# Loading every second chunk of a statistics pass from GpSimd's DMA queue

## What is computed

```python
def reference(x, w):
    v = group_norm(x)                       # 32 groups: 2 channels x 256 x 256 pixels share mean and variance
    vc = clip(v, -8, 8)
    s = max(abs(vc)).max() / 127            # ONE scale for the whole tensor
    vq = clip(round(vc / s), -127, 127) * s
    ws = mean(abs(w), per output channel)
    wq = clip(round(w / ws), -1, 1) * ws    # ternary weights
    return x + conv1x1(vq, wq)
```

## Time and profile before

| what | value |
|---|---|
| median of 3 runs | 1880.15 us (1879.89 to 1880.23) |
| the profiled execution, its own time | 1879.99 us |
| span of the profile, first to last instruction | 1878.2 us |
| busy: DVE, ACT, PE, POOL | 88%, 58%, 55%, 22% of the span |
| DMA | 797.09 MB, mean 424 GB/s over the span |
| mean granted clock of TensorE | 0.672 of full speed |

### The profile page before, as it was taken

How to read it: one execution, slowest core, us unless ns; L and a number is a source line. 1 busy time by engine, 2 the same in 40 slices (tenths; PEclk the granted TensorE clock), 3 DMA queues, 4 the chain that set the end, 5 groups by cost and what they waited for, 6 DMA issues and landing times.

```text
span 1878.2 us, 9814 instructions
## 1 busy us (share of the span) xinstructions
PE 1036.2 (55%) x2237; PEld 332.6 (18%) x2237; DVE 1646.0 (88%) x956; ACT 1085.4 (58%) x796; POOL 417.1 (22%) x139
## 2 busy tenths in 40 slices
PE   0999999999999644444434334333343333433342
PEld 0333333333333211111100000000000000000000
DVE  4999999999999999999988888888888888888885
ACT  0999899899899755455444443444434444344432
POOL 0676776767767300000000000000000000000000
PEclk9999999999999855555555555555555555555555
DMA  9999999999999979999999999999999999999998
GB/s 408 423 428 428 428 428 429 428 428 429 428 429 428 428 309 431 430 430 430 431 430 431 431 432 431 431 431 431 430 432 432 431 430 431 432 431 431 431 431 352
DMA packets 54891, 797.09 MB, mean 424 GB/s; under 512 B 6240, under 2 KB 6240, under 8 KB 6240
## 3 DMA queue, kind: packets, MB, share of 16 engines
q1 hardware_dynamic: 36288, 528.50, 66.1%
q10 hardware_dynamic: 18592, 268.48, 33.4%
HBM read 528.52 MB, written 268.44 MB: 424 GB/s over the span
## 4 chain that ended last, share of the span: by engine, by line
DMA 60%; DVE 21%; ACT 6%; issue 5%; POOL 4%; PE 3%; SPq 0%; DVEq 0%; ACTq 0%; POOLq 0%
DMA out_dram<-ring 31%; DMA ring<-in_x_dram 29%; DVE ring L513 9%; DVE square_maxs L423 5%; DVE ints L504 5%; ACT ring L297 3%; PE product L548 3%; POOL ints L273 2%; POOL levels L273 2%; ACT levels L357 2%; DVE ints L507 1%; DVE first_sq_maxs L428 1%; ACT product L290 0%; ACT ring L303 0%; DVE ints L414 0%
## 5 line engine op out<-in xcount | busy, mean ns | idle before, releaser
L583 PE MATMUL product<-ints,w_lhsT 128*128 128x512 bf16 x1024 | 482.7, 627 | 718.4 <-DVE ints L507 718.4
L357 ACT ACTIVATE levels<-ring,tile_affine 128x2048 f32<-128x2048 f32 x256 | 522.1, 2087 | 561.3 <-DMA ring<-in_x_dram 462.3
L513 DVE SCALAR_TENSOR_TENSOR ring<-product,out_scale,ring 128x2048 f32<-128x2048 f32 x256 | 600.3, 2345 | 0.1
L423 DVE TENSOR_REDUCE square_maxs<-ring 128x4096 f32 (+1 forms) x120 | 528.4, 4417 | 39.0 <-ACT ring L297 38.6
L297 ACT ACTIVATE ring<-ring,group_stats 128x4096 f32<-128x4096 f32 x120 | 443.8, 3698 | 0.0
L504 DVE TENSOR_SCALAR ints<-levels 128x2048 bf16<-128x2048 f32 x256 | 312.3, 1220 | 137.1 <-ACT levels L357 137.1
L583 PEld LDWEIGHTS product<-ints,w_lhsT 128*128 128x128 bf16 x1024 | 110.9, 130 | 1089.4 <-DVE ints L507 876.2
L273 POOL TENSOR_TENSOR levels<-ring 128x1536 f32<-128x1536 f32 x60 | 207.4, 3457 | 130.7 <-DMA ring<-in_x_dram 130.7
L544 PE MATMUL product<-ring,neg_mean 128*128 128x512 f32 x480 | 227.6, 597 | 3.9 <-ACT product L290 2.1
L273 POOL TENSOR_TENSOR ints<-ring 128x1536 f32<-128x1536 f32 x60 | 207.3, 3454 | 86.9 <-DMA ring<-in_x_dram 86.9
L507 DVE TENSOR_SCALAR ints<-ints 128x2048 bf16<-128x2048 bf16 x256 | 177.7, 694 | 8.7
(11 more groups left out here) (78 smaller groups left out, 77.3 us busy)
## 6 DMA issues: line engine op xcount, KB each, us to landing
ring<-in_x_dram SPq DMA_DIRECT2D x252, 2048.0 KB, 14.1
out_dram<-ring ACTq DMA_DIRECT2D x128, 2048.0 KB, 42.2
levels<-in_L_conv_weight_dram ACTq DMA_DIRECT2D x2, 16.0 KB, 8.7
```

The costliest lines, as they stand in the source:

```text
L357: nc.scalar.activation(levels[:, h, :], halves[:, 2 * s + h, :], ACT.Identity, bias=tile_affine[:, a, 1, :], scale=tile_affine[:, a, 0, :] ...
L423: nc.vector.tensor_reduce(square_maxs[:, bass.ds(k, 1)], ring[:, slot1(REST + g), :], AX_X, ALU.max).then_inc(maxed, 1)
L513: nc.vector.scalar_tensor_tensor(part, product[:, h, :], out_scale[:, :], part, ALU.mult, ALU.add).then_inc(combined, 1)
L583: mm = pe.matmul(product[:, h, n * BANK:(n + 1) * BANK], w_lhsT[:, :], ints[:, h, n * BANK:(n + 1) * BANK], start=True, stop=True)
```

## The change

SyncE issues the even group chunks and chunks 1 and 3. The odd ones from 5 on are issued by GpSimd, on a DMA queue of its own, each ahead of the fold of the chunk that comes three earlier (`AHEAD = 3`). GpSimd's `load1` has the same wait on `maxed` as SyncE's. Loads of GpSimd count in semaphores of their own (`pool_grouped`), so that a slot that is used by both in turn has two counts; `filled_wait` gives the semaphore and value for a chunk, and takes the place of `loads1` in GpSimd's, VectorE's and TensorE's waits. GpSimd's last turn is written out behind its loop, without loads past chunk 119.

```diff
--- before.py
+++ after.py
@@ -18,6 +18,7 @@
 SLOTS = RING1 + KEPT
 TURN = 2 * RING1
 PRE = 8
+AHEAD = 3
 BANK = 512
 GROUPS_NORM = 32
 GN_EPS = 1e-5
@@ -146,6 +147,7 @@
         kept_squared = sem("kept_squared")
         first_merged = sem("first_merged")
         grouped = [sem(f"grouped{s}") for s in range(RING1)]
+        pool_grouped = [sem(f"pool_grouped{s}") for s in range(RING1)]
         x_folded = sem("x_folded")
         part_made = sem("part_made")
         mean_kept = sem("mean_kept")
@@ -178,9 +180,19 @@
         def slot1(i):
             return (i + SHIFT) % RING1
 
-        def loads1(i, t):
-            first = [k for k in range(RING1) if slot1(k) == slot1(i)][0]
-            return t * (16 * TURN // RING1) + 16 * ((i - first) // RING1 + 1)
+
+
+        FROM_POOL = AHEAD + 1
+
+        def by_pool(g):
+            return g >= FROM_POOL and g % 2 == 1
+
+        def filled_wait(i, t):
+            g = i - REST
+            same = [k for k in range(i % RING1, i + 1, RING1) if by_pool(k - REST) == by_pool(g)]
+            if by_pool(g):
+                return pool_grouped[slot1(i)], t * 16 + 16 * len(same)
+            return grouped[slot1(i)], t * 16 + 16 * len(same)
 
 
 
@@ -211,10 +223,12 @@
                 sp.dma_start(ring[:, slot1(i), :], x_chunks[t * TURN + (TC + g)]).then_inc(grouped[slot1(i)], 16)
 
             for g in range(PRE):
-                load1(g, 0)
+                if not by_pool(g):
+                    load1(g, 0)
             with sp.Fori(0, TURNS) as t:
                 for g in range(PRE, PRE + TURN):
-                    load1(g, t)
+                    if not by_pool(g):
+                        load1(g, t)
 
             def load2(t, c):
                 s = slot2(t, c)
@@ -269,15 +283,27 @@
                     pool.wait_ge(first_summed, 1)
                 else:
                     pool.wait_ge(part_made, t * TURN + (g - 1))
-                pool.wait_ge(grouped[slot1(i)], loads1(i, t))
+                pool.wait_ge(*filled_wait(i, t))
                 pool.tensor_tensor(folded[g % 2], chunk[:, PLAIN:PLAIN + FOLD], chunk[:, PLAIN + FOLD:COLS],
                                    ALU.add).then_inc(x_folded, 1)
 
+            def load1(g, t):
+                i = REST + g
+                pool.wait_ge(maxed, t * TURN + (i - RING1 + 1))
+                pool.dma_start(ring[:, slot1(i), :], x_chunks[t * TURN + (TC + g)]).then_inc(pool_grouped[slot1(i)], 16)
+
+            def step(g, t, last=False):
+                if by_pool(g + AHEAD) and not (last and g + AHEAD >= PRE + TURN):
+                    load1(g + AHEAD, t)
+                fold(g, t)
+
             for g in range(PRE):
-                fold(g, 0)
-            with pool.Fori(0, TURNS) as t:
+                step(g, 0)
+            with pool.Fori(0, TURNS - 1) as t:
                 for g in range(PRE, PRE + TURN):
-                    fold(g, t)
+                    step(g, t)
+            for g in range(PRE, PRE + TURN):
+                step(g, TURNS - 1, last=True)
 
         @block.scalar
         def _(act):
@@ -410,7 +436,7 @@
                     dve.wait_ge(kept_loaded[c], 16)
                 else:
                     s = slot1(c - KEPT)
-                    dve.wait_ge(grouped[s], loads1(c - KEPT, 0))
+                    dve.wait_ge(*filled_wait(c - KEPT, 0))
                 then(nc.vector.scalar_tensor_tensor(pair_junk, halves[:, 2 * s, :], 0.0, halves[:, 2 * s + 1, :],
                                                     ALU.add, ALU.add, accum_out=first_sums[:, c:c + 1]))
             nc.vector.tensor_reduce(first_sum[:, :], first_sums[:, :], AX_X, ALU.add).then_inc(first_summed, 1)
@@ -539,7 +565,7 @@
                 i = REST + g
                 if not (isinstance(t, int) and t == 0 and g < 2):
                     pe.wait_ge(mean_kept, t * TURN + (g - 1))
-                pe.wait_ge(grouped[slot1(i)], loads1(i, t))
+                pe.wait_ge(*filled_wait(i, t))
                 for n in range(PLAIN // BANK):
                     pe.matmul(parts_ps[g % 2], neg_mean1[:, :], ring[:, slot1(i), n * BANK:(n + 1) * BANK],
                               start=(n == 0), stop=False)
```

## The result

The changed kernel takes **1986.93 us** (median; 1982.92 to 1988.24) against 1880.19 of the kernel before in the same sessions: ratio 1.0564, 95% interval 1.0546 to 1.0583. That is 107 us slower, where the prediction said 53 and ended its range at 1965.

What follows compares the result with a forecast made beforehand. The first pass was taken to be paced by its loads, 19.60 us per four chunks. Loop 40.5, kept reductions 9.1 and start 3.5 us sum to 53, added to 1879.99: 1933 us, range 1905 to 1965.

Steps and rivals of the forecast that it cites:

- loop with its issue, and the start: First pass: 28.5 rounds each 0.42 us plus the 1.0 us issue too long, 40.5 us; later second even fold, 3.5 us.
- kept reductions: VectorE's extra 2.28 us reduction in each of 8 turns; each of two loops pays four: 9.1 us, bounds 0 to 18.2.
- TensorE's clock: First-pass matmuls were taken to stay at 2.4 GHz; the sum had no cost for a falling clock.
- rival 4: TensorE's pauses of some 2 us per chunk pair drop its clock to 1.2 GHz: some 430 us more; chance 0.03.
- the loop: GpSimd's wait ahead of even folds closes a four-chunk chain through TensorE, ScalarE, VectorE: 20.02 us plus issue, against loads' 19.60.
- The start: Fold 2 waits for the first tile's third reduction, starting at 64.03 instead of 57.30 us; 3.5 us lost.
- the price c: Time GpSimd's DMA issue adds ahead of an even fold: taken as 1.0 us, bounds 0.33 to 3.46.
- Rival 1: GpSimd's issue is as cheap as SyncE's, 0.33 us: 1914 us, or 1905 with kept reductions hidden; chance 0.13.
- landings: GpSimd's loads land within 12.9 us of issue, in time for the 14 us allowed; landings at half the former 13.7.
- SyncE and the rest: SyncE's 58 removed issues of 0.333 us are worth nothing; the second pass keeps its length and only starts later.
- Folds in pairs: Sign on GpSimd: odd fold 3.5 us behind an even one, then some 7 us; four folds in 21.0 us.
- Rival 3 (not slower): GpSimd's wait is met early and loads still pace the first pass; perhaps 2.7 us less, 1877 us; chance 0.05.

Runs made afterwards that it cites:

- filled pause without kept reductions: Changed kernel with six short matmuls ahead of TensorE's wait for each even fold, and without the kept chunks' squares and reductions: 1923.76 us, ratio 1.0236.
- the filled pause: Changed kernel with six short unused matmuls ahead of TensorE's wait for the fold of each even chunk: 1940.85 us, ratio 1.0319.
- the exchanged order: Changed kernel with GpSimd's two statements swapped: first the fold, then the wait and the issue of the load three chunks ahead: 1895.95 us, ratio 1.0079.
- the older wait: Changed kernel with AHEAD = 2, so GpSimd's wait ahead of a fold is for a reduction one chunk older: 1892.37 us, ratio 1.0063.
- the wait alone: Kernel before, with GpSimd waiting for the reduction of chunk g-4 ahead of each even fold g; SyncE issues all loads: 1920.48 us, ratio 1.0219.

## Why the prediction was wrong

The terms of the sum against their runs, each as the difference of two medians:

| term | predicted us | measured us | from the medians of |
|---|---|---|---|
| loop with its issue, and the start | 40.5 + 3.5 = 44.0 | 43.3 | filled pause without kept reductions, less before (1923.76 - 1880.45) |
| kept reductions | 9.1 (0 to 18.2) | 17.1 | the filled pause, with them less without them |
| TensorE's clock | 0 (rival 4: some 430, chance 0.03) | 46.1 | changed kernel less filled pause (1986.93 - 1940.85) |
| sum | 53 | 106.5 | the kernels themselves: 106.7 |

The three measured differences share their ends, so they add up to the whole by construction, and that the sum closes proves nothing. The split also depends on the order: if the kept reductions are taken out first, the kernel gets 9.1 us slower (1996.03 - 1986.93), and the filled pause then gives back 72.3 us (1996.03 - 1923.76) and not 46.1. What stands by itself is the first row: VectorE's step `out_scale` starts at 704.1 us in the filled pause without kept reductions and at 659.9 in the kernel before, 44.2 us apart. Some of that closeness is luck: its first rounds hold one slow group (4.54 us, at 67.64), and its last rounds are shorter than 21.0 us.

**Right: the loop.** That a wait ahead of the fold closes a chain of four chunks, and that its length and not the loads sets the pace, is shown by the exchanged order and by the older wait, which undo it, and by the wait alone, which makes it without any DMA. Its predicted length, 20.02 + 1.0 us, is the 21.0 us of the undisturbed rounds. The start came as worked out too: the second even fold was put at 64.03 us and began at 63.97.

**Right: the price c.** From the reduction to the fold it was 0.21 + 1.0 us in the sum and 1.24 in the trace: 0.57 us is the row of the issue, some 0.6 passes ahead of it. The working behind it (144 packets at the fold's pace) was a guess that hit, and no run bears it out. Rival 1 says that every issue in the trace is below 0.7 us, but the earlier trace rows has one of 4.23; nothing in the sum hangs on it. The Trainium skill's 1 us (DMA: Bandwidth & Descriptors, Specifications), a latency to the first byte, happens to lie near 1.24 - 0.08 = 1.16 us; taken as a difference of 0.4 us to SyncE, as the prediction did beside its sum, it gives a c of 0.73 us where 1.24 - 0.21 = 1.03 was measured.

**Wrong: the step that set aside rival 4.** The prediction had TensorE pause "some 2 us in every pair" and held one row against a falling clock, a stretch with a busy share of 3.86 in 6 us at a granted 1.00. But 6.00 - 3.86 leaves 2.14 us there, so that row holds no pause of 3.5 us. The prediction also priced the fall as all or nothing, 430 us. Both steps failed for one reason. The two interleaved loops did not stay evenly apart. In the round shown above the fold of one loop makes TensorE wait, while that of the other is done before TensorE comes to it, so that two pauses of 2 us become one of 3.5. Behind that pause one group of three matmuls (six records) runs at 1.2 GHz, 2.65 us longer, and the clock is back before the next. The price is thus 2.65 us in a round, not a slow pass; over 28.5 rounds it would be at most 76 us. It was 46 in the changed kernel, and 72 without the kept reductions, where nearly every round is slow. It looks as if the slow group keeps the pattern alive, since it delays the leading loop and leaves the other time to catch up; that was not tried by itself.

**Mis-sized: the kept reductions.** The sum let each loop pay four of the eight, 1.14 us in the mean of a turn. With a steady clock they cost 17.1 us by the medians, near the upper bound of the prediction, 18.2, but each is not paid in full: a turn shown above is 1.65 us longer, as part of one loop's delay passes to the other. In the profiled executions 15.5 us of the difference lie ahead of `out_scale` (719.6 against 704.1 us). Most turns have those 1.65 us; one is 3.3 us longer, and why is not settled.

**Right: landings, SyncE and the rest.** Loads land 8.3 to 13.7 us after GpSimd's issue, inside the 14 us that were allowed though above the 12.9 of the prediction, and the folds hardly wait for them; the second pass kept its length within 2 us. Folds in pairs and the idle time ahead of the even ones ended by VectorE's reduction came as described. Landings at half the former 13.7 us did not come: the medians are 10.4 us on GpSimd's queue and 10.0 on SyncE's. The bandwidth was 368 GB/s over the pass and not near 400, because the rounds were longer than forecast.

**Rival 3 (not slower)** needed a chain shorter than its rows; it fell. Moving loads to a second queue brought no bandwidth in any of the runs, as the Trainium skill has it (DMA: Bandwidth & Descriptors, Issuing engines are not separate DMA queues): issuing from several engines saves issue time only. The exchanged order, with 419 GB/s against 428, agrees that nothing is gained, and even loses a little. (The chances of all cases but rival 3 add up to 0.95, and not to the 0.94 that the prediction has for slower.)

## What to carry to other kernels

A DMA issue moved to a busy in-order engine brings its wait along, and the wait stands in front of that engine's next work: look for the chain from that work back to the semaphore and hold its length against the pace, counted in chunks; here putting the issue behind the fold, or waiting for a reduction one chunk older, gave back 91 and 95 of 107 us. When a chain takes over the pace, TensorE gets pauses that it did not have, and the granted clock has to be a term of the sum, priced as the matmuls behind each pause at the lower level. A repeated small delay that a queue used to cover can come near its upper bound once nothing covers it (here 17 of 18 us).

## What the runs showed of the hardware

- The same fold matmuls ran at either level behind pauses of almost equal length: 5.49 us for six records behind 3.50 and 3.53 us in the rounds above, but 2.84 us behind 3.54 us in an earlier round of the changed kernel (timeline of TensorE). The length of the pause alone does not decide it.

```profile
157.85 2.84 PE L574 MATMUL product<-levels,neg_mean 128*128 128x512 f32 x6 [3.54 <-POOL levels L287]
```

- Six added matmuls in each second chunk, 1.5 us of work that nobody uses, made the changed kernel 46 us faster; taking work away (the kept reductions) made it 9 us slower.
- GpSimd's issue of a 2 MB load has a row of 0.57 us, against 0.33 on SyncE; behind a wait GpSimd's next instruction started 1.24 us after the reduction's end, against 0.08 to 0.24 with the same wait and no issue.
